# A bitwise search for the 408th smallest key on one Trainium2 core: two tiles to a sum, four tiles counted by ScalarE, a clamp in place of the sixteenth count

## The reference

```python
S = jax.nn.relu(att[:, 0])                 # scores of head 0, causal
S = S.at[..., 0].set(0.0) * (1.0 - jnp.eye(T))
FF = jnp.cumsum(S_shifted, axis=1)         # S moved down by one row, summed over rows
att = att - FF[:, None]
memory_budget = max(1, int(T * 0.2))       # 409
FF_mod = jnp.where(causal, FF, jnp.inf)
rank = jnp.argsort(jnp.argsort(FF_mod, axis=-1), axis=-1)
keep = rank < jnp.minimum(memory_budget - 1, i + 1)[None, :, None]   # 408 smallest
keep = keep | jnp.eye(T, dtype=bool)[None]
att = jnp.where(keep[:, None], att, -inf)
```

## Time and profile before

| | us |
|---|---|
| median of three runs | 2943.28 |
| the profiled execution | 2941.24 |
| its span (first to last instruction) | 2939.4 |
| PE busy | 2613.1 (89%) |
| DVE busy | 1845.0 (63%) |
| ACT busy | 1785.3 (61%) |
| POOL busy | 345.4 (12%) |
| L900, matmuls of the search, x2176 | 281.1 (238.4 + 42.7) |
| L910, sums of the search, x416 | 158.0 |

### The profile page before, as it was taken

How to read it: one execution, slowest core, us unless ns; L and a number is a source line. 1 busy time by engine, 2 the same in 40 slices (tenths; PEclk the granted TensorE clock), 3 DMA queues, 4 the chain that set the end, 5 groups by cost and what they waited for, 6 DMA issues and landing times. The chain is left out here.

```text
span 2939.4 us, 75860 instructions
## 1 busy us (share of the span) xinstructions
PE 2613.1 (89%) x31084; PEld 1634.9 (56%) x31084; DVE 1845.0 (63%) x5185; ACT 1785.3 (61%) x3488; POOL 345.4 (12%) x710
## 2 busy tenths in 40 slices
PE   8998978888889799999998989999999999896596
PEld 4696846666666462212122546766676767665355
DVE  6899977887887572100002657777877777763862
ACT  3585745655666328999997236766666666532331
POOL 3100042222221010000000100000000000016026
PEclk9998989999999899999999999999999999898598
DMA  3320010000010202100000010000000000303003
GB/s 116 57 39 1 2 16 17 17 16 11 11 16 11 53 1 83 54 30 1 1 1 17 1 40 7 2 8 7 2 7 7 7 2 2 97 13 50 29 15 58
DMA packets 85120, 68.23 MB, mean 23 GB/s; under 512 B 40776, under 2 KB 73688, under 8 KB 84392
## 3 DMA queue, kind: packets, MB, share of 16 engines
q1 hardware_dynamic: 76328, 57.09, 7.8%
q0 software_dynamic: 8448, 6.30, 1.5%
HBM read 47.21 MB, written 19.96 MB: 23 GB/s over the span
## 5 line engine op out<-in xcount | busy, mean ns | idle before, releaser
L1746 ACT ACTIVATE arena<-ps 128x1024 f32<-128x1024 f32 x512 | 474.1, 1281 | 25.9 <-PE ps L1696 24.0
L1197 DVE CUSTOM_DVE_ANT_0 arena<-ps,arena 128x1024 f32<-128x1024 f32 (+7 forms) x384 | 349.8, 931 | 107.4 <-PE ps L1073 91.4
L2124 DVE CUSTOM_DVE_ANT_0 arena<-ps,arena 128x512 f32<-128x512 f32 (+3 forms) x640 | 371.1, 643 | 26.7 <-PE ps L1988 25.8
L1149 ACT ACTIVATE arena<-ps 128x1024 f32<-128x1024 f32 (+3 forms) x320 | 275.3, 896 | 133.5 <-PE ps L1106 130.1
L2081 ACT ACTIVATE arena<-arena 128x1152 f32<-128x1152 f32 (+15 forms) x256 | 306.4, 1199 | 63.4 <-DVE arena L2124 63.4
L1988 PE MATMUL ps<-arena 64*128 64x512 f32 (+3 forms) x1280 | 270.4, 547 | 3.5 <-ACT arena L2057 1.1
L1707 PE MATMUL ps<-arena 128*32 128x512 f32 x2048 | 273.0, 604 | 0.0
L2019 PE MATMUL ps<-arena 128*64 128x128 f32 x4352 | 262.3, 275 | 0.0
L2019 PEld LDWEIGHTS ps<-arena 128*64 128x64 f32 x4352 | 235.3, 137 | 33.4 <-issue 28.7
L900 PE MATMUL ps<-arena 128*128 128x256 bf16 (+1 forms) x2176 | 239.0, 274 | 14.7 <-DVE arena L872 9.3
L2043 ACT COPY arena<-ps 128x512 f32<-128x512 f32 (+3 forms) x410 | 189.7, 517 | 75.9 <-PE ps L2005 73.7
(11 more groups left out here) (298 smaller groups left out, 4056.6 us busy)
## 6 DMA issues: line engine op xcount, KB each, us to landing
arena<-scr_q SPq DMA_DIRECT2D x256, 32.0 KB
scr_s<-scr_f SPq DMA_DIRECT2D x1, 4096.0 KB, 16.3
arena<-scr_k SPq DMA_DIRECT2D x32, 128.0 KB
arena<-by_head_k SPq DMA_DIRECT2D x16, 192.0 KB
arena<-scr_s SPq DMA_DIRECT2D x16, 192.0 KB, 2.5
arena<-by_head_q SPq DMA_DIRECT2D x28, 96.0 KB
by_head_k<-arena SPq DMA_DIRECT2D x5, 512.0 KB, 4.5
scr_x<-arena SPq DMA_DIRECT2D x2, 1024.0 KB, 5.3
```

Source lines behind the costliest of these rows:

```text
L1149: e.activation(turned_block(u, kc), src, ACT.Exp, scale=-1.0).then_inc(exped, 1)
L1197: e.tensor_tensor_reduce(scored_block(u, g)[:, lo:hi], PS[:, 1024 * (k % 2):1024 * (k % 2) + hi - lo], NF[t][:, lo:hi], -1.0, mxs[:, col - ...
L1746: e.activation(PTR[k % RS], PS[:, at(n):at(n) + 1024], ACT.Sigmoid, scale=float(1 / np.sqrt(8.0))).then_inc(weighed, 1)
L2124: e.tensor_tensor_reduce(slot(u, t, g)[:, lo:hi], PS[:, base(step) + 512 * g:base(step) + 512 * g + hi - lo], bias, -1.0, mxs[:, col - 1:c ...
```

## The change

1. **Two tiles to a sum.** Tiles 15, 12 (set 0) and 14, 13 (set 1) are "packs", tiles 8, 11 and 9, 10 "ones". A pack's mask is multiplied by 2048 in the matmul (weights `IDP` = 2048 x identity), and the ones' mask is added to the same PSUM columns. Tile 7 is summed alone. ScalarE's read now adds 2^23 in all (Identity with the bias column `spread` = 2^23/256), so that both counts can be read from the bits of one number: VectorE's new `unpack` masks the low 11 bits out for the ones' column. The limits of packs and ones are written for this.
2. **Four tiles counted by ScalarE.** For tiles 4, 3 and 6, 5 no mask is made and no matmul is issued. ScalarE runs Sign on `halves[t]` with `edge` as the bias and the accumulator on; `edge` is a new column that VectorE writes after each settling (`next_edge`).
3. **Settling** is four steps (`unpack`, `compare`, `raise_value`, `next_edge`), each behind one mask of the other set, from its third on.
4. **Round 15** counts nothing. `bounds` makes the smallest and the largest key with the found high half, `clamp` puts each key of `NF[t]` between them in fp32 (max, then min), to where masks lay, and ScalarE (tiles 15, 12, 11, 14, 13, 10, 9) or GpSimd (8, 7, 4, 3, 6, 5) copies the lower 16 bits to `halves[t]`. A key above becomes 0xFFFF, one below 0, so that the limit stays as it is. Clamps wait until the draw that read the same buffer is done, and masks of round 16 for the draws that used theirs.
5. Per round and set: masks go from 7 and 6 to 5 and 4 (108 blocks for 130), sums from 13 to 5, plus four signs of 640, 512, 896 and 768 columns. `built` counts 15 before the first mask (it was 4).

The diff, cut to its core:

```diff
-            sets = [[15, 12, 11, 8, 7, 4, 3], [14, 13, 10, 9, 6, 5]]
-            searched = sets[0] + sets[1]
+            ones_of, packs_of = [[8, 11], [9, 10]], [[15, 12], [14, 13]]
+            single_of, direct_of = [[7], []], [[4, 3], [6, 5]]
+            sums_of = [[(packs_of[i][x], ones_of[i][x]) for x in range(2)] + [(t,) for t in single_of[i]] for i in range(2)]
+            masked_of = [[t for x in sums_of[i] for t in x] for i in range(2)]
+            drawn_of = {"act": [15, 12, 11, 14, 13, 10, 9], "pool": [8, 7, 4, 3, 6, 5]}
+            clamped_of = [[15, 8, 12, 7, 11, 4, 3], [14, 6, 13, 5, 10, 9]]
...
+            slots_of = {"act": [(2, 3), (0, 1)] * 3 + [(2, 3)], "pool": [(4, 5), (6,), (4,), (6,), (5,), (6,)]}
+            reads = {0: [("sign", 4), ("sum", 0), ("sign", 3), ("sum", 1), ("sum", 2)], 1: [("sign", 6), ("sum", 0), ("sign", 5), ("sum", 1)]}
...
+                e.memset(spread, UNIT / 256).then_inc(built, 1)
+                e.memset(edge, float(1 << 14) - 0.5).then_inc(built, 1)
+                for i in range(2):
+                    ones, packs, direct, every = columns_of(i)
+                    e.memset(lim[:, ones], UNIT + ALL).then_inc(built, 1)
+                    e.memset(lim[:, packs], UNIT + PACK * ALL + PACK - 1).then_inc(built, 1)
...
+                e.tensor_scalar(IDP, IDN, PACK, None, ALU.mult).then_inc(built, 1)
...
+                def unpack(k, i):
+                    ones, packs, _, _ = columns_of(i)
+                    for x in reads[i]:
+                        w.wait_ge(counted, count_no[(k, i) + x] + 1)
+                    e.tensor_scalar(cnt.bitcast(I32)[:, ones], cnt.bitcast(I32)[:, packs], 0x7FF, 0x4B000000, ALU.bitwise_and, ALU.bitwise_or).then_inc(settled, 1)
...
+                def next_edge(k, i):
+                    direct = columns_of(i)[2]
+                    value = high if k < 15 else low
+                    step = float(1 << (13 - k)) - 0.5 if k < 14 else float(1 << (30 - k)) - 0.5 if k < 31 else 0.0
+                    w.wait_ge(settled, settled_no(k, i, 3))
+                    e.tensor_scalar(edge[:, direct], value[:, direct], step, None, ALU.add).then_inc(settled, 1)
...
+                def clamp(i, t):
+                    s, (kind, n, slots) = place[t], slots_at(t)
+                    w.wait_ge(settled, settled_no(14, i, 6))
...
+                    if before:
+                        wait_drawn(w, kind, before[-1])
+                    e.tensor_scalar(clamped_at(t), NF[t], highi.bitcast(F32)[:, s:s + 1], topi.bitcast(F32)[:, s:s + 1], ALU.max, ALU.min).then_inc(built, 1)
...
+                work = [(k, i, [(mask, k, i, t) for t in masked_of[i]] if k != 15 else [(clamp, i, t) for t in clamped_of[i]]) for k in range(NC) for i in range(2)]
...
+                    for n, (f, *x) in enumerate(todo):
+                        if n >= 2 and steps:
+                            steps[0][0](*steps.pop(0)[1:])
+                        f(*x)
...
+                            m = e.matmul(bank(g % 8, c1 - c0), IDP if t in packs_of[i] else IDB, tally[n % 7][:, c0:c1],
+                                         start=(t == sums_of[i][x][0] and c0 == 0), stop=(t == sums_of[i][x][-1] and c1 == W))
...
-                    e.activation(junk[n % 8], bank(n % 8, 256), ACT.Copy, accum_out=cnt[:, s:s + 1]).then_inc(counted, 1)
+                        e.copy(halves[t], clamped_at(t).bitcast(U16)[:, 0::2]).then_inc(counted, 1)
...
+                        e.activation(junk[len(read) % 4], bank(g % 8, 256), ACT.Identity, bias=spread, accum_out=cnt[:, s:s + 1]).then_inc(counted, 1)
...
+                        e.activation(signs[x], halves[x], ACT.Sign, bias=edge[:, s:s + 1], scale=-1.0, accum_out=cnt[:, s:s + 1]).then_inc(counted, 1)
...
+            def search_gpsimd(e, w):
+                for t in drawn_of["pool"]:
+                    w.wait_ge(built, clamped_no[t])
+                    e.tensor_copy(halves[t], clamped_at(t).bitcast(U16)[:, 0::2]).then_inc(f_closed, 1)
```

More of the change, by code:

```diff
@@ L828, in stage1 @@
             NC = 32
-            counts = [(k, i, t) for k in range(NC) for i in range(2) for t in sets[i]]
-            count_no = {x: n for n, x in enumerate(counts)}
-            def edges(i):
-                return place[sets[i][0]], place[sets[i][-1]] + 1
-            def settle_no(k, i):
-                return 2 * (2 * k + i + 1)
+            UNIT, PACK, ALL = 8388608.0, 2048.0, KEEP - 1
+            spread = SM[:, 624:625]
+            edge, topi = SM[:, 528:544], SM[:, 688:704].bitcast(I32)
@@ new lines, in stage1, with columns_of @@
+            counts = []
+            for k in range(NC):
+                counts += [(k, "draw", t) for t in drawn_of["act"]] if k == 15 else [(k, i) + x for i in range(2) for x in reads[i]]
+            count_no = {x: n for n, x in enumerate(counts)}
+            group_no = {x: n for n, x in enumerate(groups)}
+            SETTLES = {k: 4 if k < 14 or k > 15 else 6 if k == 14 else 0 for k in range(NC)}
+            def columns_of(i):
+                lo, mid = place[ones_of[i][0]], place[packs_of[i][0]]
+                last, hi = place[direct_of[i][0]], place[direct_of[i][-1]] + 1
+                return slice(lo, mid), slice(mid, mid + 2), slice(last, hi), slice(lo, hi)
@@ new lines, in settled_no, with slots_at, wait_drawn @@
+            def settled_no(k, i, step):
+                return sum(2 * SETTLES[x] for x in range(k)) + i * SETTLES[k] + step
+            def slots_at(t):
+                kind = "act" if t in drawn_of["act"] else "pool"
+                n = drawn_of[kind].index(t)
+                return kind, n, slots_of[kind][n]
+            def wait_drawn(w, kind, n):
+                if kind == "act":
+                    w.wait_ge(counted, count_no[15, "draw", drawn_of["act"][n]] + 1)
+                else:
+                    w.wait_ge(f_closed, NT + n + 1)
@@ new lines, in mask @@
+                def mask(k, i, t):
+                    n, s = mask_no[k, i, t], place[t]
+                    if k and k != 16:
+                        w.wait_ge(settled, settled_no(k - 1, i, 3))
+                    if n >= 7:
+                        w.wait_ge(folded, n - 6)
+                    if k == 16:
+                        for kind in ("act", "pool"):
+                            inside = [x for x, v in enumerate(drawn_of[kind]) if v == t or n % 7 in slots_at(v)[2]]
+                            if inside:
+                                wait_drawn(w, kind, max(inside))
+                    value, bit = (high, 14 - k) if k < 15 else (low, 31 - k)
+                    dst = tally[n % 7][:, 0:128 * (t + 1)]
+                    e.tensor_scalar(dst, halves[t], value[:, s:s + 1], float(1 << bit), ALU.subtract, ALU.is_lt).then_inc(masks, 1)
@@ new lines, in search_vector @@
+                work = [(k, i, [(mask, k, i, t) for t in masked_of[i]] if k != 15 else [(clamp, i, t) for t in clamped_of[i]]) for k in range(NC) for i in range(2)]
+                last = None
+                for k, i, todo in work:
+                    steps = []
+                    if last is not None and last[0] != 15:
+                        steps = [(f,) + last for f in ((unpack, compare, raise_value, bounds) if last[0] == 14 else (unpack, compare, raise_value, next_edge))]
+                    for n, (f, *x) in enumerate(todo):
+                        if n >= 2 and steps:
+                            steps[0][0](*steps.pop(0)[1:])
+                        f(*x)
+                    for f, *x in steps:
+                        f(*x)
+                    last = (k, i)
@@ new lines, in search_vector @@
+                for f in (unpack, compare, raise_value):
+                    f(*last)
+                w.wait_ge(settled, settled_no(NC - 1, 1, 3))
+                e.tensor_copy(lowi, low).then_inc(built, 1)
+                w.wait_ge(built, N_BUILT + 13 + 1)
+                e.tensor_tensor(thr.bitcast(I32)[:, 0:13], highi[:, 0:13], lowi[:, 0:13], ALU.bitwise_or).then_inc(built, 1)
+                w.wait_ge(built, N_BUILT + 13 + 2)
+            N_BUILT = 4 + 2 * 2 + 4 + 1 + 2
+            clamped_no = {t: N_BUILT + n + 1 for n, t in enumerate(clamped_of[0] + clamped_of[1])}
```

125 lines of the change are left out of this document (69 added, 56 removed).

## The result

| | kernel before | changed kernel |
|---|---|---|
| median, us | 2946.06 (6 runs, 2940.08 to 2949.52) | 2929.09 (6 runs, 2927.63 to 2932.59) |
| ratio to before | 1 | 0.9946, 95% interval 0.9935 to 0.9957 |
| profiled execution, us | 2941.24 (span 2939.4) | 2928.62 (span 2926.9) |
| search, first mask to the first instruction behind it | 251.67 | 232.58 |
| a normal round | 7.10 | 6.75 |

The changed kernel is faster by 17.0 us, about 0.5%. The forecast was 25.7 us less and a time of 2917; 2929 lies inside the range on record (2905 to 2933), near its slow end, and outside the forecast's own band (2911 to 2924).

What follows compares the result with a forecast made beforehand. TensorE bounded normal rounds (7.09 of 7.10 us), VectorE round 15. Setup, cold rounds, 6.40 us rounds, round 14, a 19.0 us phase and the last round summed to 225.95 against 251.67, -25.7, hence 2917 us; range 2905 to 2933.

Steps and rivals of the forecast that it cites:

- the forecast's own band: The time expected if no rival came true: 2911 to 2924 us, chance 0.58.
- The forecast's own branch: Search: rounds of 6.3 to 6.55 us and a round 15 phase of 17 to 22 us, chance 0.58.
- signs of being wrong: Search: a table load, a granted clock below 1.00, a round over 6.7, or GpSimd draws that overlap clamps.
- rival 1: Normal rounds: VectorE becomes the bound, small steps cost 0.20 instead of 0.08; rounds 6.7 to 6.9, time 2927, chance 0.18.
- first clamp to first mask of 16: Round 15: 19.0 us, bounds 17.0 and 24 to 26; GpSimd's draws start only where VectorE pauses; 14 without that rule.
- last round and tail: End of the search up to L1172: 8.85 us, ending with five dependent steps of 0.20.
- hand-overs: Chain of a normal round: 0.06 from mask to TensorE, 0.04 on to ScalarE, 0.03 from ScalarE to the unpack.
- The chain: Normal round: a loop through all three engines, 3.38 us to set 0's unpack, 2.98 to set 1's; 6.40 taken.
- Rivals 1 and 3: Normal rounds: small steps at full 0.20 (2927, chance 0.18); sums at 0.37 with draws at the plain slope (2910, chance 0.07).
- Rival 2: Round 15: clamps gain nothing, GpSimd's draws at 2.7 ns a column; phase 25 to 26 us, time 2923, chance 0.10.
- Cold starts: Rounds 0 and 16: TensorE starts at half clock; 9.05 us each, bounds 8.2 and 9.6.
- rival 4: ScalarE in the search: table loads of 1.28 us between Sign and Identity; rounds of 16.0, time about 3200, chance 0.03.

## Why the prediction was right, and where it was off

The direction, the part that gains, and the kind of bound were right; the gain was forecast 8.7 us too large, of which 6.9 are in the search by the profiled executions. It was right by its range more than by its number. The forecast's own branch (6.3 to 6.55 a round) missed, and one of its signs of being wrong came true, a round over 6.7. The time came out where rival 1 had it (2927, rounds of 6.7 to 6.9), and the range held because it reached up to that rival, whose mechanism was not the cause. (The chances of rivals 1 to 3 and of the forecast add up to 0.93; the prediction has 0.92.) It was also luck that three terms gave back 3.5 us of what the rounds lost. By the terms of the sum, in the profiled execution:

| term | forecast | measured | difference |
|---|---|---|---|
| setup | 0.5 | 0.29 | -0.2 |
| round 0 | 9.05 | 8.59 | -0.5 |
| rounds 1 to 13 | 13 x 6.40 = 83.2 | 13 x 6.74 = 87.6 | +4.4 |
| round 14 | 6.7 | 7.09 | +0.4 |
| first clamp to first mask of 16 | 19.0 | 16.67 | -2.3 |
| round 16 | 9.05 | 8.36 | -0.7 |
| rounds 17 to 30 | 14 x 6.40 = 89.6 | 14 x 6.77 = 94.8 | +5.2 |
| last round and tail | 8.85 | 9.43 | +0.6 |
| sum | 225.95 | 232.8 | +6.9 |

- **The loop: mis-sized hand-overs.** The chain was the right one (unpack, mask 12, tiles 12, 11, 7, sum, unpack), and its sizes held to a few hundredths once both waits were gone (6.40). The failed terms are the hand-overs, 0.06 and 0.03 by the forecast, 0.146 and 0.13 measured, four of them in a round: 0.34 x 27 = 9 us. Rival 1 had named the evidence, that waits on several semaphores are issued apart, but looked for its price on VectorE's own sum, and not on the loop. VectorE did not become the bound: it was 81% busy, and a small step between masks cost 0.08.
- **VectorE's steps, sums and signs.** Small steps at 0.08, sums at 0.47 (0.46 forecast), signs of 0.71 to 1.04 as forecast. Rivals 1 and 3 fall with them.
- **Round 15.** The forecast took GpSimd's draws at 1.3 ns a column; they run at 0.87 to 0.92, near the plain slope of the earlier trace rows (0.83). That the engines exclude each other was right, but the forecast made 5 us of it (19 with, 14 without). Measured, VectorE is held for 3.6 us; what the phase would be without exclusion no run shows. Moving the draws to VectorE, which then has them to do itself, gives 0.6 (16.67 to 16.06). With 19.0 against 16.67 the phase gave back 2.3 of what the loop lost. In this trace the phase ends on ScalarE, as forecast: the mask at 231.52 starts 0.03 behind its last draw. Rival 2 (25 to 26 us) was far off.
- **Cold starts.** 8.59 and 8.36 instead of 9.05: the price lay between the value taken and the lower bound.
- **Table loads** (rival 4): none in the search, though ScalarE goes back and forth between signs and sums eight times in each round.
- **Behind the search.** The search ends 18.8 us earlier, the profiled execution is only 12.6 shorter, the medians 17.0. The part behind the search took 2576.5 us before (2939.4 - 362.94) and 2582.8 after (2926.9 - 344.14). Most of these 6 us is the choice of execution: the profiled one of the kernel before lies 4.8 us under its median, that of the changed kernel 0.5. In the twelve experiments, on other chips, the instructions behind the search are the same; there the part lies between 2601.8 and 2610.1, without order by where the search ends (2603.2 with an end at 319.75, 2601.8 with one at 401.92). So nothing shows a loss that the change causes there.
- **What the sum had left out.** The forecast took the place of the settling as given, since it stood in the diff. It showed neither as a cost nor as a rival, though the chain was computed with "two masks ahead of it". It is the largest single term that the runs found: 0.5 of 6.40 us a round, or 0.7 of the changed kernel's 6.75, more than all hand-overs together (0.35).

The phase of round 15 takes 15.2 to 15.3 us in the four kernels without signs and 16.0 to 16.7 with them. The traces show where this comes from: the first mask of round 16 has another buffer. With nine masks a round it has number 135, hence buffer 2 of 7, which ScalarE's last draw (tile 9) still reads; VectorE stands still for 1.32 us until that draw is done (the line at 231.52 above). With 13 masks it has number 195, hence buffer 6, and starts right behind the last clamp, before ScalarE's two draws of 235.75 are through. VectorE and ScalarE in the kernel with the clamps alone and the settling last:

```profile
237.00 0.74 DVE L950 TENSOR_SCALAR arena<-arena 128x2048 bf16<-128x2048 uint16 x1
...
235.75 2.62 ACT L1001 COPY arena<-arena 128x1408 uint16<-128x1408 uint16 x2 [0.44 <-DVE arena L935]
```

What stays open: whether the order of TensorE's two waits alone is worth its share of the hand-overs. The clamps alone with the early settling were 12 to 23 us slower than the kernel before, where their search is 10.8 longer; the search also started 2.5 us later in that trace, and together the 13.3 lie inside. First masks start anywhere from 111.26 to 114.36 in the experiments, without order by the edit; why, no run shows.

## What to carry to other kernels

When a change frees several engines at once, write the loop that closes a round as a chain and ask two things of it: how many waits each instruction on it has, and which of them is fulfilled last (a second wait cost 0.09 us a time here where the added instruction held that one, and most of it was hidden once the loop was not the bound), and how much independent work each in-order queue has ahead of its waiting instruction (one more mask in front of the settling was worth 0.5 us a round). Parts of such a change may lose alone and gain together, since each moves the bound to another engine: packing alone, with the settling last, left VectorE full at 7.36, signs alone, with the early settling, left ScalarE full at 7.54, and only both together, with the settling from the fourth mask on, reach TensorE's 5.9.

## What the hardware showed that was not expected

- An instruction that waits for two conditions had one of 50 ns beside it in the records that only waits. Where that one held the condition that was fulfilled last, the start came 0.09 to 0.10 us later behind it: 130 to 133 ns against 31 to 34 (ScalarE to VectorE), 146 against 57 ns (VectorE to TensorE). Where it held the other one, as in the kernel before, the matmul started 56 to 57 ns behind its mask in spite of it.
- VectorE and GpSimd hold each other up both ways: a VectorE step of 6 columns took 1.12 us instead of 0.16, ending 0.03 behind the GpSimd copy beside it. In the same stretch the clamps of 1664 and 1536 columns, which had started first, kept their full speed, and the copy waited; clamps that came behind a copy were held (768 columns 1.28 us instead of 0.68).
- A strided 16-bit copy ran at 0.87 to 0.92 ns a column on GpSimd, about 0.83 on ScalarE (1898 ns for 2048 columns), and 0.52 on VectorE (755 ns for 1152 and 423 for 512 columns).
